# Prologue reordered, expert combine one step earlier, and the last block of expert outputs moved from behind the last attention products to step 31 and between them

## The reference

```python
xn = _layernorm(x)
qkv = einsum('bse,he->bsh', xn, w_qkv); q, k, v = split(qkv, 3)
probs = softmax(einsum('bqh,bkh->bqk', q, k) / sqrt(8))      # 2048 x 2048, one head
attn = einsum('bqk,bkh->bqh', probs, v)
attn = swapaxes(attn, 1, 2).reshape(...) @ w_proj.T + b_proj
t = xn @ W_in + b_in
route = top2 of softmax(t @ W_gate + b_gate), renormalised    # 8 experts
eout = relu(t @ W1[e] + b1[e]) @ W2[e] + b2[e]                # 128 -> 512 -> 128
moe = sum_e route[:, e] * eout_e @ W_out + b_out
out = x + attn + moe
```

## Time and profile before

| quantity | value |
|---|---|
| three runs | 248.6, 248.9, 247.85 us (median 248.6) |
| profiled execution | 246.94 us, of which the span 245.2 us |
| PE busy | 231.1 us (94%) |
| DVE / ACT / POOL busy | 137.2 / 111.8 / 141.2 us |
| the chain that ended last | PE 78%, DVE 7%, POOL 6%, issue 3%, DMA 3%, ACT 2% |
| mean granted clock of PE | 0.993 |

### The profile page before, as it was taken

How to read it: one execution, slowest core, us unless ns; L and a number is a source line. 1 busy time by engine, 2 the same in 40 slices (tenths; PEclk the granted TensorE clock), 3 DMA queues, 4 the chain that set the end, 5 groups by cost and what they waited for, 6 DMA issues and landing times.

```text
span 245.2 us, 4891 instructions
## 1 busy us (share of the span) xinstructions
PE 231.1 (94%) x1756; PEld 218.8 (89%) x1756; DVE 137.2 (56%) x330; ACT 111.8 (46%) x265; POOL 141.2 (58%) x163
## 2 busy tenths in 40 slices
PE   7798699799999999999999999999999989999994
PEld 7697487699999998899999999999989879899993
DVE  4954877464244252444544444444587786986652
ACT  2554233242333423435444444445556546656561
POOL 3109303898888860146655666565078888888800
PEclk9999979999999999999999999999999999999999
DMA  6799900101111113012222222221111111313111
GB/s 184 290 316 337 315 12 11 55 32 45 43 44 35 43 43 86 13 32 67 75 68 75 66 75 70 75 64 47 42 35 44 35 43 43 90 32 82 38 43 43
DMA packets 23047, 19.54 MB, mean 80 GB/s; under 512 B 3280, under 2 KB 19696, under 8 KB 22768
## 3 DMA queue, kind: packets, MB, share of 16 engines
q1 hardware_dynamic: 20000, 14.71, 19.8%
q0 software_dynamic: 2048, 4.20, 6.0%
q10 hardware_dynamic: 976, 0.33, 0.5%
HBM read 10.97 MB, written 8.26 MB: 78 GB/s over the span
## 4 chain that ended last, share of the span: by engine, by line
PE 78%; DVE 7%; POOL 6%; issue 3%; DMA 3%; ACT 2%; ACTq 1%; POOLq 0%; DVEq 0%
PE ps L1044 14%; PE ps L1030 14%; PE ps L910 11%; PE ps L848 5%; PE ps L789 5%; PE ps L790 5%; PE ps L791 5%; POOL wtab L380 5%; PE ps L797 3%; DVE part_max L598 3%; DMA w_raw<-in_L_attn_w_proj_dram 2%; PE ps L923 2%; PE ps L919 2%; PE ps L920 2%; PE ps L1018 2%
## 5 line engine op out<-in xcount | busy, mean ns | idle before, releaser
L343 POOL COPY wst<-wtab 128x1156 f32 x39 | 44.9, 1151 | 39.6 <-DVE y_sb L735 39.6
L455 ACT ACTIVATE pf<-ps 128x512 f32<-128x512 f32 x64 | 38.1, 595 | 35.8 <-PE ps L791 35.6
L598 DVE TENSOR_REDUCE part_max<-ps 128x1 f32<-128x1024 f32 x32 | 39.0, 1223 | 15.4 <-PE ps L848 15.2
L380 POOL DMA_INDIRECT wtab<-slots_out,slots x32 | 33.8, 1056 | 16.1 <-DMA slots_out<-y_sb 8.4
L353 POOL DMA_INDIRECT slots_in<-hl,slots x32 | 31.4, 983 | 20.0 <-DVE slots L674 13.0
L727 DVE TENSOR_SCALAR mid<-ps,wst 128x128 f32<-128x128 f32 x78 | 23.8, 347 | 32.7 <-PE ps L1030 32.7
L789 PE MATMUL ps<-q_hi,xnT_hi 128*128 128x256 f32 x128 | 41.5, 325 | 0.5 <-ACT q_hi L441 0.5
L1044 PE MATMUL ps<-wst,mid 128*128 128x128 f32 x312 | 41.3, 275 | 0.7 <-DVE x_sb L625 0.7
L1030 PE MATMUL ps<-xgT,wst 128*128 128x128 f32 x312 | 41.3, 275 | 0.0
L1044 PEld LDWEIGHTS ps<-wst,mid 128*128 128x128 f32 x312 | 38.0, 192 | 0.8 <-ACT mid L495 0.8
L1030 PEld LDWEIGHTS ps<-xgT,wst 128*128 128x128 f32 x312 | 38.0, 192 | 0.2
(11 more groups left out here) (145 smaller groups left out, 348.3 us busy)
## 6 DMA issues: line engine op xcount, KB each, us to landing
wtab<-in_L_ffn_W_dram SPq DMA_DIRECT2D x16, 256.0 KB, 6.2
xg<-slots_in SPq DMA_DIRECT2D x39, 64.0 KB, 1.9
slots_out<-y_sb SPq DMA_DIRECT2D x39, 64.0 KB, 1.5
slots_in<-wst SPq DMA_DIRECT2D x2, 1024.0 KB, 4.9
x_sb<-in_L_attn_x_dram SPq DMA_DIRECT2D x4, 256.0 KB, 4.9
out_dram<-x_sb SPq DMA_DIRECT2D x3, 256.0 KB, 2.5
wtab<-in_L_ffn_b_dram SPq DMA_DIRECT2D x1, 512.0 KB, 7.4
slots_in<-hl,slots POOLq DMA_INDIRECT x32
```

Of the source, the lines that this page charges most:

```text
L343: pool.tensor_copy(wst[:, t % 4, :], wtab[:, bass.ds(experts[t], 1), :].rearrange("p a n -> p (a n)")).then_inc(Z["staged"], 1)
L380: pool.indirect_dma_start(out=z[:, j, c, :], out_offset=None, in_=slots_out, in_offset=bass.IndirectOffsetOnAxis(ap=slots[:, c, j:j + 1], ...
L455: act.activation(pf[:, i % 3, :], ps[:, st_bank(i), :], ACT.Exp).then_inc(Z["pf_done"], 1)
L598: dve.tensor_reduce(part_max[:, g % 2, m // 2, m % 2:m % 2 + 1], ps[:, b:b + 2, :], AX.XY, ALU.max).then_inc(Z["max_read"], 1)
```

## The change

Prologue: half as many `keep_warm` products (24 to 12, 4 to 2, 4 to 2); all four transposes stand ahead of any `project_in`; `project_in(1)` moves behind the first two score pairs and `project_in(3)` goes to banks 2 and 3 behind the last pair; ScalarE copies `hl` block 3 after `row(0)`; VectorE's `bn_aggr` is spread over the blocks. Second half: `combine(j)` stands one step earlier, `weigh(j)` one gather earlier. Block 3 is transposed in step 31, and projected between the last two `values`; its `moe_add` stands ahead of `scale_out`.

```diff
-        return [j for j in range(NT) if 5 + (13 * (j + 1)) // 8 == s]
+        return [j for j in range(NT) if 4 + (13 * (j + 1)) // 8 == s]
-    BLOCK_AT = {14: 0, 22: 1, 26: 2}
+    BLOCK_AT = {14: 0, 22: 1, 26: 2, 31: 3}
...
         def hl_banks(r):
-            b = 4 if r == 0 else 0
+            b = (4, 0, 0, 2)[r]
...
-                if j >= 2:
-                    weigh(j - 2)
-            weigh(NT - 2)
+                if j >= 1:
+                    weigh(j - 1)
             weigh(NT - 1)
...
             xT_high(2)
+            xT_high(3)
             hl_copy(0)
-            xT_high(3)
-            hl_copy(1)
...
             q_high(0)
+            hl_copy(1)
             hl_copy(2)
-            hl_copy(3)
...
             row(0)
+            hl_copy(3)
...
-            cT_copy(NR - 1)
...
+            def ln_aggregate(r):
+                dve.wait_ge(Z["ln_link"], TB * (r + 1))
+                for j in range(TB * r, TB * (r + 1)):
+                    last = dve.bn_aggr(mv[:, j, :], stats[:, j, :])
+                return last
...
             normalise(2)
-            xT_low(0)
             normalise(3)
             dve.wait_ge(Z["hw_hi_ready"], 1)
             dve.tensor_tensor(hw_lo[:, :], ps[:, UB, 0:HW], raw(hw_hi[:, :]), ALU.subtract).then_inc(Z["hw_lo_ready"], 1)
+            xT_low(0)
...
+            moe_add(NR - 1)
             for r in range(ROUNDS[NG - 1]):
                 scale_out(NG - 1, r)
-            moe_add(NR - 1)
...
-                pe.wait_ge(Z["xT_lo"], max(r + 1, 2))
-                if r >= 2:
-                    pe.wait_ge(Z["hl_ready"], r)
+                pe.wait_ge(Z["xT_lo"], (1, NR, NR, NR)[r])
+                if r == 2:
+                    pe.wait_ge(Z["hl_ready"], 2)
+                if r == 3:
+                    pe.wait_ge(Z["max_read"], 3)
...
-            keep_warm(24)
+            keep_warm(12)
             xn_transpose(0)
-            keep_warm(4, 4)
+            keep_warm(2, 4)
             xn_transpose(1)
-            keep_warm(4, 4)
+            keep_warm(2, 4)
             xn_transpose(2)
+            keep_warm(2, 4)
+            xn_transpose(3)
             pe.wait_ge(Z["hw_lo_ready"], 1)
-            keep_warm(2, 4)
             project_in(0)
-            xn_transpose(3)
-            project_in(1)
...
             pair(0, 1)
+            project_in(1)
+            pair(0, 2)
+            pair(0, 3)
             project_in(2)
-            pair(0, 2)
             project_in(3)
-            pair(0, 3)
-            pe.wait_ge(Z["hl_ready"], NR)
+            pe.wait_ge(Z["hl_ready"], 3)
...
+                if i == 2:
+                    pe.wait_ge(Z["hl_ready"], NR)
...
             values(LAST - 2)
+            moe_project(NR - 1)
             values(LAST - 1)
-            moe_transpose(NR - 1, FIRST_PAIR[NG])
             for r in range(ROUNDS[NG - 1]):
                 out_rows(NG - 1, r)
-                if r == 0:
-                    moe_project(NR - 1)
```

More of the change, by code:

```diff
@@ L546, in ln_stats @@
                     count["ln"] += 1
+            def ln_aggregate(r):
[3 more added lines that the diff above has]
+                return last
             for r in range(NR):
                 ln_stats(r)
[L550 to L553, removed]
+                if r >= 1:
+                    ln_aggregate(r - 1)
+            link("ln", ln_aggregate(NR - 1))
             link("ln", dve.tensor_scalar(veps[:, :], mv[:, :, 1], EPS, None, ALU.add))
```

## The result

| quantity | before | after |
|---|---|---|
| median of 15 runs each, taken in turn | 246.89 us (246.4 to 248.9) | 244.97 us (243.39 to 246.71) |
| ratio after/before | | 0.9899, 95% interval 0.9873 to 0.9926 |
| profiled execution | 246.94 us | 245.20 us, of which the span 243.5 us |
| PE / DVE / ACT / POOL busy | 231.1 / 137.2 / 111.8 / 141.2 us | 228.5 / 136.8 / 111.6 / 140.3 us |

The change makes the kernel about 1% faster: 2.5 us by the ratio, 1.9 by the medians, 1.74 between the profiled executions. The forecast was a change of -2.0 to 246.6 us. The size of the change came out nearly as forecast.

The account below looks back on a forecast made before the run. TensorE was taken to bound the kernel, its chain of waits leaving it only in the prologue, around 178 to 197 us and the last 6 us. -2.9 - 1.0 + 1.9 = -2.0 us, from 248.6 to 246.6; range 244.9 to 248.3.

Parts of the forecast that it names:

- term 1: Prologue: fewer fillers and new order bring the routing 3.65 us earlier, less 0.8 for a slow clock: -2.9 us.
- term 2: Second half: earlier weighing and combining remove TensorE waits of 0.33, 0.91, 0.21, leaving one of 0.4: -1.0 us.
- The bound of 1.3: Prologue: net clock loss of 1.3 us in the bound that, with routing 0.4 later, gave -1.9.
- the lower bound on the wait: Second half, step 8: VectorE's wait for POOL's `weigh(2)`, taken at 0.4 us, bounds 0 and 1.0.
- Term 3: End: block 3's transposes and projection ahead of the last `values`, with a 0.9 wait for `combine(15)`: a loss of +1.9 us.
- Rival 1: No slow stretch that costs, or cheaper transposes at the end: prologue at its full -4.1, 245.4 us; chance 0.13.
- Rival 2: Fewer fillers let the clock fall in the prologue too, costing 1.7 us on TensorE's queue: 248.3 us; chance 0.12.
- Rival 3: Prologue gives nothing, as the four maxima and the banks they free still decide: 249.5 us; chance 0.05.
- Rival 4: Gathers landing later than 4.1 us hold up POOL; at 4.5 TensorE waits in step 31: +4.3, 250.9 us; chance 0.04.
- the signs named for a wrong forecast: Routing starting later than 27 us, TensorE waiting over 1.5 us in step 31, or the clock falling before 25 us.

Follow-up runs that it names:

- e12: e5 with weighing and combining back at their places in the kernel before: 242.64 us, ratio 0.982.
- e5: Changed kernel with 13 filler products ahead of `prefix` and block 3 transposed and projected at the end again: 241.49 us, ratio 0.9793.
- e4: Changed kernel with 13 filler products in PE's wait between `scores(1)` and `prefix`: 243.38 us, ratio 0.9855.
- e7: e4 with block 3's transposes moved between the first two of the last three `values`: 242.91 us, ratio 0.9847.
- e11: e10 without the 12 filler products ahead of the first transposes too: 242.13 to 250.19 us in twelve runs, median 246.67.
- e1: Kernel before with the prologue's part of the change alone: 243.46 us, ratio 0.9862.
- e8: e4 with the prologue's fillers raised to 24, 4, 4, 4 products from 12, 2, 2, 2: 247.25 us, ratio 1.0024.
- e10: e5 without the three `keep_warm(2, 4)` between the groups of transposes: 241.52 us, ratio 0.9774.
- e3: Changed kernel with block 3 transposed and projected at the end again: 243.38 us, ratio 0.9833.
- e9: Kernel before in its old order, with `keep_warm` 24, 4, 4 cut to 12, 2, 2: 244.41 us, ratio 0.9902.

## Why the prediction was right in its change and wrong in its time

**The step that failed is the last one of the sum.** It read: "The profiled execution took 246.94, 1.66 below the median of 248.6, so it would take 244.9, and the median becomes 246.6." That treats 1.66 us as a steady offset between the profiled execution and the others. It was not. Over 15 runs before's median is 246.89: the profiled execution was an ordinary one, and the three runs of the table (248.6, 248.9, 247.85) came from the upper part of its range. The other 12 of the 15 have a median of 246.74. In the 51 runs of the kernel before in the three sessions the mean clock is 0.993 in 27, at 246.2 to 247.2 us, and 0.984 to 0.986 in 15, at 247.4 to 248.7. With the profiled execution as the base, the forecast for an execution of that kind stands on record at 244.9; measured were 245.20 in the profile and 244.97 in the median. The error of 1.63 us in the time is the base's 1.71 (248.6 - 246.89), less 0.08 from the change (-1.92 by the medians).

That the change itself agrees so closely, -1.92 against -2.0, is in part luck: -1.68 in the profiles and -2.5 by the ratio are as good readings of it, and one term inside it was mis-sized, the clock in term 1.

The terms, in the two profiled executions:

| term | forecast | measured in the profiles | how |
|---|---|---|---|
| 1, prologue | -2.9 | -2.44 | last `y_sb` 173.27 against 175.71 |
| 2, weigh and combine | -1.0 | -1.11 | last `low` 232.95 against 236.50 is -3.55, less -2.44 |
| 3, block 3 | +1.9 | +1.87 | last add 240.57 against 242.25 is -1.68, less -3.55 |
| sum | -2.0 | -1.68 | spans -1.7 |

(Of term 2, 0.91 is there at `o_sb` in step 11, 193.60 against 196.95; the other 0.2 is the last wait of the earlier trace rows, 0.21.)

**Term 1.** Each place came out within 0.15 us: `q_project` 17.21 (17.3 forecast), first pair 18.27 (18.4), routing 26.07 (26.2), `prefix` 30.39 behind 2.82 idle (30.5 behind 3). The term that was mis-sized is the clock: 0.8 net forecast, 3.78 - 2.44 = 1.34 measured. Of that, 1.54 less the 0.36 that it had cost before is lost by `pair(1, 0)`, the rest by `y_sb`. I had let part of the slow stretch fall into the idle time; it began with `prefix`, so nothing of it was free. The bound of 1.3 was the better figure. What I had no view of is that the fall comes only in some executions. By the mean clocks it came in 11 of after's 15 runs and cost 1.6. Before, it costs little where it comes (the runs at 0.998 and 0.999 lie at 246.1 to 246.6, those at 0.993 at 246.2 to 247.2), since the slow products fill a wait.

**Term 2.** The wait I took at 0.4 was 0.24 on VectorE and 0.46 on PE; the three others went. 1.15 us between e12 and e5, 1.11 in the profiles: right. (`weigh(j)` moved by one tile, that is by two gathers, as the sum has it.) I had not expected POOL to wait for a landing at all; it did, 1.09 us at 230.58, for `combine(15)` at 233.56. The weighing still ended 2.3 us before that, so it moved nothing. The stretched gather was read from one row, and that reading is too short: of before's 32 gathers seven took 1.24 to 1.46 us, each of them beside a `low`, but twelve others that ran beside a `low` for 0.5 us or more took 0.94 to 1.03 (POOL's times are rough in the profile). What stretches a gather is open, and so is the lower bound on the wait that rested on it.

**Term 3.** 1.89 us between the medians of e4 and e5 (1.5 by their ratios), +1.87 in the profile, +1.9 forecast. The wait ahead of the transposes was 0.73 (0.9 forecast); from the last score product to the `ut` copy it takes 4.72 us (232.96 to 237.68; 4.7 forecast), in e5 2.73. e7 takes a quarter of it back by shortening the wait; the rest, as far as it is known, is work moved out of waits that hid it into a queue that was full.

**The rivals.** Rival 1 (no costly slow stretch) is, by the clocks, what happens in 4 of 15 runs of after, and in all of e4: 243.4 there. On the right base its own figure is 243.7. Rival 2 (the clock falls in the prologue) did not occur in the profiles with 12 filler products, and does without any (e11). Rival 3 is refuted by e1. Rival 4 needed landings above 4.1 us; the longest was 3.9 and the median 2.6. (Its "slower than before from about 4.25" should be 4.34 by its own numbers: 14 x 0.24 = 3.3 on 234.7 is 238.0, 2.0 behind the 236.) None of the signs named for a wrong forecast showed: the routing started at 26.07, PE waited 0.73 in step 31, and the clock did not fall before 25 us in after's profile.

What stays open: why the same idle time of 2.8 us is followed by the slow clock in one execution and not in the next. The idle time starts at the same place in after's and e1's profiles (27.6 us), and nothing seen in them tells the two apart. What brings before's second group, at 0.984 to 0.986, was not traced either, nor why the first three runs all lay so high.

## What to carry to other kernels

Forecast a change from one profiled execution, but look at how the kernel's times scatter before taking a base: where the clock falls in some executions, three runs can all lie on one side, here by more than half of the effect. Before taking work out of a serial tail, ask what waits it stands in; moved into a full queue it costs about its whole length and any wait that comes with it (1.9 us here). A wait of some 3 us that a change opens on PE can be filled with throwaway products of its length (worth 1.6 us here, and a narrow scatter), while fillers that delay a result on the path are the first thing to cut.

## What the runs showed that I had not expected

- Fillers of the same kind were worth opposite things: 24 + 4 + 4 + 4 products cost 3.9 us against 12 + 2 + 2 + 2 (e8 against e4), the three small ones are worth nothing (e10), the last 12 save up to 8.7 us in a bad execution (e11).
- An idle time of 2.8 us ahead of `prefix` was followed by a clock of 0.54 in after's profile and by 1.00 in e1's. After's times fall into groups 1.6 us apart: 243.39 to 243.55 (4 runs), 244.82 to 245.29 (9), 246.59 and 246.71 (2).
- In e3's profile the slow level held from 30.5 past 36, in after's only to 34. By the groups of e3's runs that costs a further 1.0 to 1.6 us.
- Half the fillers without the new order (e9) come out the same as half the fillers with it wherever the clock falls; the order pays only once its wait is filled or the clock happens to stay up.
